# Transformer block on one core: the prologue of the attention rebuilt (norm bounds in blocks, order of stores, loads and first shifts)

## The reference, cut to what matters

```python
x = L0_attn_x                                   # (1, 2048, 128) f32
xn = (x - mean) / sqrt(var + 1e-5)
qkv = xn @ W_attn.T + b_attn                    # 16 heads of 8
att = softmax(where(causal, q @ k.T / sqrt(8), -inf))
y = (att @ v) @ W_proj.T + b_proj
probs = softmax(xn @ choice_w.T)                # 8 experts
G, I = top_k(probs over the 2048 tokens, 512)   # per expert
moe[I] += G * (silu(xn[I] @ w1[e]) @ w2[e])
out = x + y + moe
```

## Time and profile before

| | us |
|---|---|
| median of 3 runs | 351.4 |
| the runs | 351.24, 352.75, 351.4 |
| the profiled execution, whole | 350.45 |
| its span from the first to the last instruction | 348.5 |
| matrix engine busy / ScalarE busy in the span | 304.0 / 288.6 |
| first exponential of the main loop starts | 44.45 |

### The profile page before, as it was taken

One profiled execution on the slowest core, in us unless ns is written; L12 is line 12 of the kernel. 1 busy time (PEld: TensorE's weight loads), 2 busy tenths in 40 slices (PEclk: granted clock), 3 DMA queues, 4 the chain that ended last, 5 costly groups with the idle time before them and its releaser, 6 DMA issues.

```text
span 348.5 us, 6205 instructions
## 1 busy us (share of the span) xinstructions
PE 304.0 (87%) x2430; PEld 104.1 (30%) x2430; DVE 186.7 (54%) x406; ACT 288.6 (83%) x328; POOL 123.2 (35%) x122
## 2 busy tenths in 40 slices
PE   0885859888899899996999899999999999999983
PEld 0452712211212332231133332323133141423262
DVE  5939974776867879640316453261236443433054
ACT  1197757889999999995998889898999989899920
POOL 8420200750000000038748667384827015242500
PEclk9999557999999999998999999999999999999999
DMA  6036269488101211014334524143434204050319
GB/s 181 0 115 187 66 210 372 137 209 104 56 23 48 87 46 56 3 39 116 106 105 70 153 40 92 23 71 95 67 89 81 73 30 66 6 91 0 32 40 264
DMA packets 35745, 31.78 MB, mean 91 GB/s; under 512 B 3704, under 2 KB 30544, under 8 KB 35712
## 3 DMA queue, kind: packets, MB, share of 16 engines
q1 hardware_dynamic: 27248, 24.00, 21.7%
q0 software_dynamic: 8464, 7.35, 14.0%
HBM read 14.36 MB, written 16.97 MB: 90 GB/s over the span
## 4 chain that ended last, share of the span: by engine, by line
PE 53%; DVE 17%; ACT 14%; issue 8%; DMA 5%; POOL 1%; SPq 1%; ACTq 0%; DVEq 0%
PE bank L1234 25%; PE bank L1216 13%; ACT probs L743 11%; PE bank L1290 5%; DVE probs L1057 4%; PE bank L1283 3%; PE bank L1178 2%; DVE passed L942 1%; POOL parts L627 1%; DVE y_acc L1078 1%; DMA xn<-total_dram 1%; PE bank L1276 1%; DVE above L954 1%; PE bank L1142 1%; DVE xn L776 1%
## 5 line engine op out<-in xcount | busy, mean ns | idle before, releaser
L743 ACT ACTIVATE probs<-bank 128x1024 f32<-128x1024 f32 x272 | 255.5, 1062 | 22.7 <-PE bank L1216 21.9
L1234 PE MATMUL bank<-probs,v_grp 128*32 128x512 f32 (+3 forms) x1280 | 149.8, 550 | 9.8 <-DVE probs L1057 9.0
L1216 PE MATMUL bank<-q_aug,k_aug 51*128 51x512 bf16 (+3 forms) x640 | 89.0, 357 | 3.1 <-ACT probs L743 2.0
L652 POOL DMA_INDIRECT total_dram<-m_space,token x32 | 52.0, 1626 | 69.4 <-DVE m_space L1043 62.1
L1057 DVE TENSOR_TENSOR probs<-probs,causal 128x512 f32<-128x512 f32 (+1 forms) x80 | 45.1, 586 | 41.8 <-ACT probs L743 41.8
L627 POOL DMA_INDIRECT parts<-xn_dram,token x32 | 32.8, 1026 | 86.3 <-DVE gate L1024 76.8
L1216 PEld LDWEIGHTS bank<-q_aug,k_aug 51*128 51x128 bf16 x640 | 22.2, 94 | 117.2 <-ACT probs L743 91.5
L1234 PEld LDWEIGHTS bank<-probs,v_grp 128*32 128x32 f32 x1280 | 27.2, 109 | 61.2 <-issue 31.8
L1033 DVE COPY m_space<-bank 128x512 f32<-128x512 f32 x16 | 11.0, 689 | 27.2 <-PE bank L1283 27.2
L1043 DVE TENSOR_TENSOR m_space<-bank,gate 128x512 f32<-128x512 f32 x8 | 5.5, 689 | 30.4 <-PE bank L1290 30.4
L1078 DVE COPY y_acc<-bank 128x512 f32<-128x512 f32 x16 | 11.0, 690 | 18.6 <-PE bank L1234 18.6
(11 more groups left out here) (133 smaller groups left out, 212.9 us busy)
## 6 DMA issues: line engine op xcount, KB each, us to landing
y_dram<-y_acc SPq DMA_DIRECT2D x16, 256.0 KB, 2.4
q_aug<-product_dram SPq DMA_DIRECT2D x32, 96.0 KB
k_aug<-product_dram SPq DMA_DIRECT2D x32, 96.0 KB, 2.2
w_x<-in_L_ffn_w_dram POOLq DMA_DIRECT2D x16, 128.0 KB, 2.8
product_dram<-parts SPq DMA_DIRECT2D x4, 384.0 KB, 3.0
product_dram<-parts SPq DMA_DIRECT2D x6, 256.0 KB, 3.2
product_dram<-parts SPq DMA_DIRECT2D x2, 768.0 KB, 4.8
x_sb<-in_L_attn_x_dram SPq DMA_DIRECT2D x4, 256.0 KB, 3.9
```

The lines of the kernel that those rows point to most:

```text
L652: pool.indirect_dma_start(total_dram, bass.IndirectOffsetOnAxis(ap=token[:, e, t:t + 1], axis=0), y_exp[:, e % 2, t, :], None, compute_op= ...
L743: act.activation(dst, src, ACT.Exp, scale=SCALE).then_inc(s_exp, 1)
L1216: last = pe.matmul(scores[(NU * g + u) % SB][:, a, at:at + width], k_aug[HEAD_ROWS[a], p, j * P:(j + 1) * P], q_aug[HEAD_ROWS[a], p, c * N ...
L1234: last = pe.matmul(acc[32 * h:32 * h + 32, first:first + width], v_grp[:, g % 2, j, h, :], probs[:, (NS * g + k) % PB, h, at:at + width], ...
```

## The change

- The bound on a block of 128 partitions. The squares are summed with a wider selector (`head_sel`, 128 x 240), of which eight tiles of 128 tokens times 16 heads fill 128 partitions of one bank: 32 bf16 matmuls of 128 x 128 in place of 8 of 16 x 512. One reduction gives the largest per tile, head and side (`most`, 128 x 4); four transposes put it into one row of one partition; there the running largest over the 16 tiles is made in a copy and four steps (shifts by 1, 2, 4, 8 tiles) of 1 x 256, the flag in three more, and two small matmuls put the key maxima back on partitions (`key_col`). ScalarE's root then takes them as its scale (two instructions of 128 x 128), and one VectorE instruction makes all shifts. GpSimd's part in it is gone.
- First parts straight from the bank. ScalarE writes part 0 from the product (`first_part`) and squares that; VectorE makes the remainder from the bank, the bias and part 0 (`remainder`), so `kT` and `qT` hold remainders from the start. Part 1 is cast on VectorE for chunks 0 and 1, on ScalarE for 2 and 3. GpSimd's remainders are gone.
- `PIECES` are chunk 0, chunk 1, chunks 2 and 3. Stores are in the order of the diff below; the whole of xn goes to memory after the loads of chunk 3.
- The shifts of chunk 0 don't go through memory: four transfers from `shift` to the rows of `q_aug`, two on SyncE's queue, two on ScalarE's, the latter behind the loading of the table for the exponentials. Chunk 1's are loaded through memory by GpSimd. Zeros and ones of the shift rows come by DMA, and GpSimd's filling of `k_aug` is gone. `future`, `tri`, `lane`, `sel` and `sel_sum` are set by GpSimd after xn is whole.
- The matrix engine multiplies the identity with itself 14 times before the weights are there (`WARM`) and 4 times behind their transposes (`WARM_2`). Values and router logits are made after the norms, between the steps of the bound. All 16 tiles of values have to be copied before the matrix engine loads the flag.
- The weight transposes are copied by ScalarE in place of VectorE; x and weights are loaded in another order.

```diff
-    PIECES = [(0, N), (N, T)]
+    PIECES = [(0, N), (N, 2 * N), (2 * N, T)]
...
+        def first_shifts(queue, p):
+            for a in reversed(range(2)):
+                h = 2 * p + a
+                queue.dma_start(q_aug[HALF * a + ROWS:HALF * a + ROWS + 1, p, chunk(0)],
+                                shift[h:h + H * (TPC - 1) + 1:H, 0, :]).then_inc(s_stage_q[0], 16)
...
+            store_both(0, 0)
+            store_both(1, 0)
+            store_both(0, 1)
+            store_both(0, 2)
+            store_both(1, 1)
+            store_both(1, 2)
+            sp.wait_ge(s_dram[0], 16 * N_PIECE_DMAS)
             stage_products(sp, 0, chunk(0), s_stage_q[0])
             stage_k(sp, 0, chunk(0), s_stage_k[0])
-            store_shifts(1, s_dram[1])
+            sp.wait_ge(s_shift, 1)
+            first_shifts(sp, 1)
+            for i in range(2):
+                sp.dma_start(shift_rows[:, 0, i * T // 2:(i + 1) * T // 2].rearrange("h (m t) -> m h t", t=P),
+                             shift[:, i, :]).then_inc(s_shiftsent[i], 16)
+            sp.wait_ge(s_dram[1], 16 * N_PIECE_DMAS)
+            stage_products(sp, 0, chunk(1), s_stage_q[1])
+            stage_k(sp, 0, chunk(1), s_stage_k[1])
+            for part in range(3):
+                store_both(2, part)
...
-            pool.memset(k_aug[:, :, :], 1.0).then_inc(s_const, 1)
...
+            pool.wait_ge(s_shiftzero, 16)
+            pool.wait_ge(s_shiftsent[0], 16)
+            stage_shifts(pool, 0, chunk(1), s_shifts_1)
...
             deviation(0)
+            act.wait_ge(s_wt_ps, 1)
+            act.activation(wT[:, :, :], flat(0).rearrange("p (i c) -> p i c", i=4), ACT.Copy).then_inc(s_wt, 1)
+            act.activation(cwT[:, :], flat(1)[:, 0:E], ACT.Copy).then_inc(s_wt, 1)
+            copy_xnT(0)
             deviation(1)
-            copy_xnT(0)
             deviation(2)
             deviation(3)
...
+            act.wait_ge(s_norm, 2 * NC)
+            act.wait_ge(s_keycol, 1)
+            for i in range(2):
+                act.activation(bound[:, i, :], flat(7)[:, (2 + i) * P:(3 + i) * P], ACT.Sqrt,
+                               scale=key_col[:, i:i + 1]).then_inc(s_mb, 1)
 
             act.wait_ge(s_ident, 1)
             act.activation(unread[:, :], ident[:, 0:1], ACT.Exp)
-            for side in range(2):
-                cast(side, 1, 1)
+            second_part(3, 1)
+
+            act.wait_ge(s_shift, 1)
+            first_shifts(act, 0)
...
             moments(0)
+            layernorm(0)
+            moments(1)
+            moments(2)
+            layernorm(1)
+            moments(3)
+            layernorm(2)
+            layernorm(3)
...
             pe.wait_ge(s_ident, 1)
+            for i in range(WARM):
+                pe.matmul(flat(6)[:, 0:P], ident[:, :], ident[:, :], start=True, stop=True)
             pe.wait_ge(s_w, 48)
```

More of the change, by code:

```diff
@@ L394, in stage_k @@
                   .then_inc(done, 16)
-        def chunk(c):
-            return slice(c * N, (c + 1) * N)
         @block.sync
@@ L855, in _ @@
[L855 to L857 removed]
+            group_values(0)
             dve.wait_ge(s_flag, 1)
@@ new lines, in _ @@
+            queries_and_keys(2)
+            queries_and_keys(3)
+            pe.wait_ge(s_const, 3)
+            norms(0)
+            norms(1)
+            norms(2)
+            norms(3)
+            logits(0)
+            pe.wait_ge(s_rem[0][2], 1)
+            pe.wait_ge(s_rem[1][2], 1)
+            pe.wait_ge(s_cols, 1)
+            for side in range(2):
+                for i in range(2):
+                    last = pe.transpose(flat(0)[0:1, (2 * side + i) * P:(2 * side + i + 1) * P],
+                                        most[:, side, i:i + 1], ident[:, :])
```

475 lines of the change are left out of this document (248 added, 227 removed).

## The result

Four executions of the changed kernel took 339.31, 340.08, 343.71 and 344.39 us, median 341.9; the kernel before took 351.5 (351.24 to 352.75). The ratio is 0.972 [0.968, 0.976]. The profiled execution is the one of 340.08: 10.4 less than the profiled one of before, where the sum said 7.9. What the medians hide is the spread: 5.1 us between four executions of one kernel. The kernel before had 1.5 beside it, and 1.9 to 3.4 in the longer series beside the experiments (one execution of 391.3 left out), so part of it is not new.

The account below looks back on a forecast made before the run. Main loop close to full on TensorE (87% busy) and ScalarE (83%), so an earlier prologue end moves everything behind it; 350.45 - 7.9 = 342.5, median 0.95 above, 343.5; forecast 341.5 to 345.5 (0.50), range 339.8 to 348.0.

Parts of the forecast that it names:

- the sum: Whole kernel: 350.45 less 7.9 from chunk 1's earlier start gives 342.5 for a profiled-like execution, median 343.5.
- The warm-up: Front, TensorE: 7.1 us until full speed, taken over 3.6, so the 28 warm instructions run to 9.2.
- the new wait: Prologue: ScalarE's fourth root, ahead of its first part, waits for VectorE's moments(3); keys' first part at 15.0.
- The branch on TensorE: Before the first scores: flag load and branch cost 2.0 after values are copied at 35.2, bounds 0 and 3.
- The masks: VectorE, before chunk 1: masks start at 41.5; chunk 1's first exponential at 43.9 full clock, 45.1 half clock.
- Transfers hide: Chunk 0's shifts land by 36.5, covered by values and branch with 0.7 to spare; chunk 1's loads and stores hide.
- rival 5: First shifts: the two queues save nothing, at most 0.6 for two issues; inside the forecast, no separate chance.
- The clock: TensorE before chunk 1: half level again around 40 to 47, so chunk 1 at 45.1, 7.9 earlier.
- Rival 1: Clock holds at 2.4 GHz through the masks; chunk 1 starts 9.1 earlier, median 341.4; chance 0.19.
- Rival 2: Half clock inside the bound, falling at about 22 to 27; first scores at 41.5, gain 3.9, 347.5; chance 0.18.
- Rival 3: Main loop gives the gain back through last piece's stores or GpSimd's work on chunk 1's masks; 350 to 352; chance 0.08.
- The same times less a constant: Sign for the main loop: from the second group on, times as before less a constant; wrong if it shrinks after chunk 1.

Follow-up runs that it names:

- experiments 1 and 2: Changed kernel without its unused fallback and branch (340.4 us, ratio 0.968); changed kernel with TensorE's wait for copied values behind its branch (342.9 us, 0.973).
- experiment 3: Changed kernel with first shifts all issued by SyncE (341.9 us), chunk 0's shifts through memory (342.1 us), or last piece's stores held until first scores (342.9 us).
- experiments 2, 5 and 6: Early-fall traces: values' wait behind the branch (342.9 us); spreading matrix made later (343.1 us); no fallback, four unread filler products on TensorE (339.1 us).
- late_spread: Changed kernel with GpSimd's making of the spreading matrix moved behind the first four experts' fetches: 343.1 us, ratio 0.973.
- v_after_branch: Changed kernel with TensorE's wait for the copied values moved behind its branch: 342.9 us, ratio 0.973.
- all_sp: Changed kernel with all four transfers of the first shifts issued by SyncE, none by ScalarE: 341.9 us, ratio 0.972.
- hold_stores: Changed kernel with SyncE's six stores of the last piece held back until the first scores are there: 342.9 us, ratio 0.977.
- no_warm: Changed kernel without its 14 + 4 warm-up products on TensorE: 341.4 us, ratio 0.969.
- no_branch: Changed kernel with the fallback left out on all engines, so no flag load and no branch: 340.4 us, ratio 0.968.
- nb_late: Changed kernel without its fallback and with GpSimd's selections for the spread matrix after its first four fetches: 338.0 us, ratio 0.964.
- shifts_mem: Changed kernel with chunk 0's first shifts stored to memory and loaded again by SyncE, in place of direct transfers: 342.1 us, ratio 0.973.

## Why the prediction was right, and where it was not

**The time** was right: 341.9 for 343.5, with the mechanism that the sum followed (ScalarE freed in the prologue, a short bound, masks earlier). That mechanism is read from the rows; no run puts the old bound or the separate first parts back, so their shares of the gain were not measured one by one. Two terms of the sum were mis-sized and cancel in part, which is luck, and two of its rivals are seen in some executions.

**The warm-up, 1.7 too long.** Between 7.1 and 3.6 us until full speed I took 7.1. The warm products' 28 end at 7.5 rather than 9.2; 3.6 would have given 7.3. (They take 4.73 to 6.25 in the eleven traces, so neither number is a constant.) Everything behind shifts by as much: keys' first part 13.2 for 15.0 (with the new wait where I put it, 2.50 for VectorE's moments), last square 23.9 for 26.1, shifts 30.3 for 32.3. The steps between were as forecast: small steps 0.44 for 0.43, third parts 2.4 for 2.3.

**The branch on TensorE, 3.0 too short.** I took 2.0 from VectorE's row and bounded it at 3; it is 5.0 from the last copy of the values (33.4) to the first score (38.4). The step that failed is the upper bound: a row of another engine does not bound it. The hint stood in the same sentence, that before the branch had been passed while logits were queued; the change's wait for the values takes that cover away, and experiments 1 and 2 price it: 4.96 and 0.73. What stands behind it is the fetch of a 16 KB packet of code (experiment 3). VectorE's own branch was 1.3 for 2.1.

The two give a first exponential at 39.0 for 38.1. **The masks** at 40.1 were 1.4 earlier than forecast: VectorE was ready at 39.4, 2.1 early, from the shorter warm-up and its own shorter branch, and then waited 0.66 for an exponential, which TensorE's branch had made late. Chunk 1 came at 44.1 for 45.1.

**Transfers hide**, as said: no DMA released a score, and the second queue (rival 5) was worth nothing. I had the order on ScalarE's queue wrong: the shifts were issued at 30.36, during the table load, not behind it; they were covered all the same.

**The clock.** The fall before chunk 1 came, at 34.6 to 44.8 where the forecast had 40 to 47; the products of step 0 ran at half speed as forecast (1.94). Rival 1 (it holds) was not seen in any trace. Rival 2 (half clock inside the bound) is what the early-fall traces of experiments 2, 5 and 6 show, with logits at twice their time and first scores at 42.4 in one of 344.3, and the changed kernel's executions of 343.7 and 344.4 have a mean clock as low as late_spread's and v_after_branch's (0.956, for 0.955 and 0.957, against 0.975 for the two shorter ones); they have no trace, and a second fall behind 57 lowers the mean too (0.961 in all_sp and hold_stores). So rival 2 may hold in two of four executions, at 344 rather than 347.5, and then its 0.18 was low; this is not shown.

**Rival 3** (given back through GpSimd's work) had a chance of 0.08 and named chunk 1's masks. The mechanism exists, at 52 to 57 and at a price of 2 to 3 us instead of all, and the profiled execution escaped the fall of clock, by luck as it seems. "The same times less a constant" held only there.

**The rest of the gain**, 10.2 of span against 8.9 at chunk 1, was no term of the sum. ScalarE's timelines have it by the twenty-sixth exponential (75.92 before, 65.60 now): 1.0 by the thirteenth (61.39, 51.46), where before waited 0.90, 0.29 and 0.37 with the clock low until 56.7, and 0.4 more by 76. Behind that the difference stays between 10.2 and 10.6. That the higher clock removed these waits was not tested.

## What to carry to other kernels

A branch over code that never runs can cost an engine a fetch of code, and costs it little only while it still has work queued ahead: keep the last blocking wait behind the branch, not in front, and take its price from a row of that engine. Where a wait reads `issue`, look for `instruction` packets in the list of DMA queues. When one kernel's executions spread by more than the effect asked about, look at where the granted clock falls in each trace before believing any median; here four executions of one kernel lie 5 us apart, and no edit moved the median by as much. A gain at the start is kept only if the next collision (here GpSimd's selections beside VectorE's small steps) doesn't land on the new times, so look there first when an earlier start gives nothing.

## What was new about the hardware

- TensorE's branch: 4.93 to 5.00 us of idle time in four traces behind a wait, 5.79 and 7.00 in two more, 0.73 and 0.85 where the wait stood behind it; no shorter at a DMA share of 0.41 than at 1.02. In these eight the next matmul starts 1.67 to 1.77 after a 16 KB packet of instructions has ended, and VectorE's next instruction 1.9 to 2.0 after one of 8 KB (its branch: 1.27 to 4.83). In no_warm TensorE waits 1.33 before the first scores, runs seven or eight matmuls of them and waits 3.65 more, with the packet at 43.26 to 44.20 in that second wait. When a fetch begins is open.
- Between two executions of the same instructions the clock fell at 28.6 in one and stayed at the 2.4 GHz level past 33 in the other, with TensorE busy throughout the window from 28 to 32 in both and the same busy times in the 4 us ahead of it.
- One idle time of 1.4 to 1.7 and one of 0.86, with a single product of 0.34 between them, were each time followed by the 1.2 GHz level (no_branch, all_sp, hold_stores); 0.44 and 0.87 were not (nb_late), nor 0.91, 0.27 and 0.86 (the changed kernel), nor 1.54 alone (shifts_mem, at 50.44).
- ScalarE's DMAs went out at 30.36 while its table load (30.02 to 31.30) was running.
